# Two MLPs become streams of their own, stage A's mean matmuls take whole tiles, and the order is written anew

## The reference, cut to what matters

```python
x = _L0_xattn_ref(x, ctx_2048, ...)        # norm over all of (64, 256), 8 heads
x = _L1_xattn_ref(x, ctx_2048, ...)        # 16 heads, keys from the normed ctx
x = _L2_xattn_ref(ctx_2048, x, ...)        # keys from ctx and from x, then an MLP
x = _L3_xattn_ref(x, ctx_2048, ...)        # self attention, cross attention, MLP
...
mu = jnp.mean(input, axis=(1, 2), keepdims=True)      # layer 0
var = jnp.var(input, axis=(1, 2), keepdims=True)
...
out = rmsnorm(attn_out, postnorm_w)                   # layer 2
out = jax.nn.gelu(out @ mlp_w1 + mlp_b1) @ mlp_w2 + mlp_b2
return out + residual
...
ln_out = layernorm(x, ln3_s, ln3_b)                   # layer 3
mlp_out = gelu(ln_out @ w1 + b1) @ w2 + b2
return x + mlp_out
```

## Time and profile before

| what | value |
|---|---|
| time, median of 3 runs | 1334.38 us (1333.51 to 1335.9) |
| the profiled execution | 1336.17 us, its span 1334.1 us |
| TensorE busy | 1257.8 us, 94% |
| VectorE, ScalarE, GpSimd busy | 1041.4, 883.5, 568.4 us |
| mean granted TensorE clock | 0.98 of full |
| moved | 25.78 MB, mean 19 GB/s |

### The profile page before, as it was taken

The page is one execution under the profiler, slowest core; times in us unless marked ns, Lnnn a source line. Parts: engine busy times, 40 slices in busy tenths (PEclk is TensorE's granted clock), DMA queues, the critical chain, the costliest instruction groups (busy, mean ns, idle before and its releaser), DMA issues.

```text
span 1334.1 us, 35216 instructions
## 1 busy us (share of the span) xinstructions
PE 1257.8 (94%) x13116; PEld 964.1 (72%) x13116; DVE 1041.4 (78%) x2450; ACT 883.5 (66%) x2299; POOL 568.4 (43%) x977
## 2 busy tenths in 40 slices
PE   6999999999999999999999999999999999989675
PEld 4767678677686877777686777868777776868564
DVE  4778887878878788897888788787878778695753
ACT  3676666776875757676666866866677766756352
POOL 2552643463444436444454534444353453351421
PEclk9999999999999999999999999999999999989896
DMA  8100000000000000000000000000000000000000
GB/s 323 30 14 17 3 22 8 18 6 11 14 12 17 7 23 7 7 17 12 18 7 10 18 3 23 11 18 7 7 22 6 19 10 2 1 7 5 2 5 4
DMA packets 23589, 25.78 MB, mean 19 GB/s; under 512 B 10624, under 2 KB 22912, under 8 KB 23168
## 3 DMA queue, kind: packets, MB, share of 16 engines
q1 hardware_dynamic: 23424, 23.55, 5.6%
HBM read 21.44 MB, written 2.10 MB: 18 GB/s over the span
## 4 chain that ended last, share of the span: by engine, by line
PE 77%; DVE 9%; ACT 6%; issue 5%; POOL 2%; DMA 1%; SPq 0%; POOLq 0%; DVEq 0%; ACTq 0%
PE bank L678 9%; PE bank L504 8%; PE bank L944 8%; PE attended L633 8%; PE bank L953 8%; PE bank L618 7%; PE bank L712 5%; PE bank L684 5%; PE bank L493 4%; PE bank L738 3%; PE bank L701 3%; PE bank L725 3%; PE bank L671 2%; PE bank L415 2%; PE bank L729 2%
## 5 line engine op out<-in xcount | busy, mean ns | idle before, releaser
L605 POOL TENSOR_SCALAR p_a<-p_a,rec_a 128x256 f32<-128x256 f32 x512 | 245.8, 499 | 177.3 <-DVE rec_a L560 176.9
L591 ACT ACTIVATE p_a<-bank,nmax_a 128x256 f32<-128x256 f32 x512 | 237.5, 477 | 68.9 <-DVE nmax_a L554 68.1
L554 DVE TENSOR_REDUCE nmax_a<-bank 128x2 f32<-128x512 f32 x256 | 167.6, 679 | 13.0 <-PE bank L504 12.4
L618 PE MATMUL bank<-ident,p_a 128*128 128x128 f32 x1024 | 146.5, 278 | 8.7 <-POOL p_a L605 3.3
L504 PE MATMUL bank<-k_a,q_a 64*128 64x256 f32 x1024 | 141.6, 399 | 2.0 <-ACT p_a L666 0.6
L618 PEld LDWEIGHTS bank<-ident,p_a 128*128 128x128 f32 x1024 | 114.4, 142 | 39.8 <-issue 32.4
L633 PE MATMUL attended<-p_a,v_a 128*64 128x256 f32 x1024 | 135.0, 391 | 1.3 <-ACT p_a L666 1.3
L504 PEld LDWEIGHTS bank<-k_a,q_a 64*128 64x128 f32 x1024 | 90.6, 186 | 32.8 <-issue 24.6
L666 ACT ACTIVATE p_a<-bank 128x512 f32<-128x512 f32 x128 | 76.4, 600 | 52.3 <-PE bank L618 51.9
L591 ACT ACTIVATION_READ_ACCUMULATOR p_a<-bank,nmax_a 128x1 f32 x512 | 106.4, 208 | 0.0
L633 PEld LDWEIGHTS attended<-p_a,v_a 128*64 128x64 f32 x1024 | 64.2, 137 | 49.3 <-issue 21.3
(11 more groups left out here) (248 smaller groups left out, 3002.2 us busy)
## 6 DMA issues: line engine op xcount, KB each, us to landing
wb<-in_wb SPq DMA_DIRECT2D x1, 4096.0 KB, 12.8
wc<-in_wc SPq DMA_DIRECT2D x1, 4096.0 KB, 23.9
xc<-in_x SPq DMA_DIRECT2D x16, 128.0 KB, 2.7
xc<-in_ctx SPq DMA_DIRECT2D x16, 128.0 KB, 2.9
c_top<-in_ctx SPq DMA_DIRECT2D x16, 128.0 KB, 2.9
k_c<-in_ctx SPq DMA_DIRECT2D x16, 128.0 KB, 2.1
res_a<-in_x SPq DMA_DIRECT2D x16, 128.0 KB, 2.1
out<-y_out SPq DMA_DIRECT2D x16, 128.0 KB, 1.7
```

What stands on the lines that cost most here:

```text
L554: dve.tensor_reduce(nmax_a[:, n, e, :], ps[:, :].rearrange("p (q k) -> p q k", q=KT), AX.X, ALU.max, negate=True).then_inc(A.s["max"], 1)
L591: last = act.activation(p_a[:, j % 2, n, e, qt, :], ps[:, qt * D:(qt + 1) * D], ACT.Exp, bias=nmax_a[:, n, e, qt:qt + 1], accum_out=sum_a[ ...
L605: last = pool.tensor_scalar(p_a[:, j % 2, n, e, qt, :], p_a[:, j % 2, n, e, qt, :], rec_a[:, n, e, qt:qt + 1], 1.0, ALU.mult, ALU.mult)
L618: last = nc.tensor.transpose(ps[:, kt * D + qt * P:kt * D + (qt + 1) * P], p_a[:, j % 2, n, e, qt, kt * P:(kt + 1) * P], ident[:, :])
```

## The change

It has three parts. The MLP of E becomes a stage G and that of F a stage H, with own letters in the strings, own tiles for the hidden values (`g_hid`, `h_hid`), the normed input (`g_xn`, `h_xn`), its transpose and the residual; the sum `x6` gets a tile of its own too, and `wide` now lies in `qT`. The waits follow: what writes `x6` waits for G of the pair before, what writes `x5` for H. The two mean matmuls use a 128 x 128 tile of 1/64 with operands whose lower 64 partitions were set to zero once, at the start; the averages are read from the first 64 partitions as before. And `ORDER` and `BANK` are written anew. The title of the change says that the search for the order priced TensorE's changes of tile shape.

```diff
-    "e": (("xT",), ("q",), ("k",), ("v",)) + attention_fills(2) + (("nT0",), ("h0",), ("h1",), ("y",), ()),
+    "e": (("xT",), ("q",), ("k",), ("v",)) + attention_fills(2),
     "c": (("nT0",), ("q",), ("k",), ("v",)) + attention_fills(1),
-    "f": (("nT0",), ("q",)) + attention_fills(1) + (("nT1",), ("h0",), ("h1",), ("y",), ()),
+    "f": (("nT0",), ("q",)) + attention_fills(1),
+    "g": (("nT0",), ("h0",), ("h1",), ("y",), ()),
+    "h": (("nT0",), ("h0",), ("h1",), ("y",), ()),
...
-        "cbcccbceeeeeecccceeeeefeffeeeeefffckfcccfcfffccfccffffffffffff"),
+        "cbcehceeeehehcccceeeeefeffeggggffgfkfccchchchhccccfffffffhhhhh"),
...
-        mean_of_all = sb("mean_of_all", [S, S])
+        mean_of_all = sb("mean_of_all", [P, P])
...
-            T.wide = t("wide", [P, KT, P])
+            T.wide = T.qT
...
+        def mlp_tiles(T):
+            t = lambda n, shape: sb(f"{T.name}_{n}", shape)
+            T.hid, T.res = t("hid", [P, MT, P]), t("res", [P, D])
...
-        x2, x3, x4, x5 = (sb(f"x{n}", [P, D]) for n in range(2, 6))
-        x6 = E.xT[:, :, :].rearrange("p f q -> p (f q)")
+        x2, x3, x4, x5, x6 = (sb(f"x{n}", [P, D]) for n in range(2, 7))
...
-            filled(N, mm(ps[0:S, 0:2], mean_of_all[:, :], mv_a[:, :, 0], start=True, stop=True), i, "mean")
+            filled(N, mm(ps[:, 0:2], mean_of_all[:, :], mv_a[:, :, 0], start=True, stop=True), i, "mean")
...
+            if i == 0:
+                dve.memset(mv_a[S:P, :, :], 0.0)
+                dve.memset(small_a[S:P, :, :], 0.0)
...
+            def x6_free(eng):
+                if i:
+                    eng.wait_ge(G.s["xn"], G.at(i - 1, "xn", 1))
+            yield from pe_attention(E, i, ((K, ("v", 2)), (E, "v")), x6_free)
+
+        def pe_g(i):
+            yield from pe_norm(G, i, 0, "nT0")
```

More of the change, by code:

```diff
@@ L309, in norm_tiles @@
             T.stats, T.mv, T.eps, T.msq, T.rstd = t("stats", [P, 6]), t("mv", [P, 2]), t("eps", [P, 1]), t("msq", [P, 1]), t("rstd", [P, 1])
[L310 to L314, removed]
+            T.xnT = t("xnT", [P, KT, P])
+            T.xn = T.yT[:, :, :].rearrange("p f q -> p (f q)") if T is not K and T in (C, F) else t("xn", [P, D])[:, :]
         def attention_tiles(T, blocks):
@@ L427, in dve_n @@
             for n in range(2):
-                dve.bn_aggr(mv_a[:, n, :], stats_a[:, n, :]).then_inc(N.s["mv"], 1)
+                dve.bn_aggr(mv_a[0:S, n, :], stats_a[:, n, :]).then_inc(N.s["mv"], 1)
             yield
-            mean, dev, sq, var, eps, scale, shift, bias = (small_a[:, k, :] for k in range(8))
+            mean, dev, sq, var, eps, scale, shift, bias = (small_a[0:S, k, :] for k in range(8))
             ps = wait_fill(N, dve, i, "mean")
@@ L435, in dve_n @@
             written(N, dve, i, "mean")
-            dve.tensor_tensor(dev, mv_a[:, :, 0], mean, ALU.subtract).then_inc(N.s["dev"], 1)
+            dve.tensor_tensor(dev, mv_a[0:S, :, 0], mean, ALU.subtract).then_inc(N.s["dev"], 1)
             yield
@@ L786, in dve_attention @@
                 dve.wait_ge(T.s["res"], T.at(i, "res", 1))
-                residual = T.res[:, 0, :]
+                residual = T.res[:, :]
             ps = wait_fill(T, dve, i, "p")
@@ L866, in dve_norm @@
             dve.wait_ge(T.s["rstd"], T.at(i, "rstd", n + 1))
-            if n:
-                written(T, dve, i, f"nT{n - 1}")
+            if i and T in (G, H):
+                wait_fill(T, dve, i - 1, "nT0")
             if rms:
@@ L1078, in x3_free @@
                     eng.wait_ge(C.s["res"], C.at(i - 1, "res", 1))
-            yield from pe_mlp(E, i, WBt, "nT0", x3_free)
+            yield from pe_mlp(G, i, WBt, "nT0", x3_free)
         def dve_e(i):
@@ L1161, in pe_f, with x5_free, pe_h @@
             pe_project_T(F, i, "q", WCt["q1"], F.xnT)
-            yield from pe_attention(F, i, ((K, ("v", 4)),), lambda eng: None)
-            yield from pe_norm(F, i, 1, "nT1")
+            def x5_free(eng):
+                if i:
+                    eng.wait_ge(H.s["xn"], H.at(i - 1, "xn", 1))
+                    eng.wait_ge(H.s["res"], H.at(i - 1, "res", 1))
+            yield from pe_attention(F, i, ((K, ("v", 4)),), x5_free)
+        def pe_h(i):
+            yield from pe_norm(H, i, 0, "nT0")
             def stored_before(eng):
@@ L1167, in stored_before @@
                     eng.wait_ge(stored, 16 * i)
-            yield from pe_mlp(F, i, WCt, "nT1", stored_before)
+            yield from pe_mlp(H, i, WCt, "nT0", stored_before)
         def dve_f(i):
```

235 lines of the change are left out of this document (124 added, 111 removed).

## The result

The changed kernel takes 1304.26 us, median of 4 runs (1303.31 to 1305.18), against 1335.14 us (1333.51 to 1336.49) for the kernel before.

The account below looks back on a forecast made before the run. TensorE's own list was taken as the bound, with a softmax-and-norm chain in the last 100 us. Terms -8.0 + 3.2 - 3.5 - 1.5 - 3.0 = -12.8 us gave 1321.6 us from the median, range 1306 to 1336.

Parts of the forecast that it names:

- Fewer changes of shape: Along TensorE's list, 773 changes of shape become 687, 86 at 0.093 us each: -8.0 us.
- The mean matmuls: The 32 products on whole 128*128 tiles take up to 0.10 us more each on TensorE: +3.2 us.
- Work moved into the gaps of the end: In the last pair, 5.9 us of work moves behind E's begin, where TensorE idles: net -3.5 us.
- the clock: In the last pair's stretch from E on, a busier TensorE may keep 2.4 GHz rather than 1.2: -1.5 us.
- Own streams and tiles: MLPs and tiles freed from E of the next pair; only TensorE's waits can change: -3 us, bounds -15 and +25.
- ScalarE's loads: 12 fewer table loads on ScalarE, 15.4 us less work there, hidden beside VectorE's work: nothing, 3 us at most.
- Rival 1: B's softmax becomes a wait in every pair, 1.7 us in each of 15 pairs: +25.5, 1347 us; chance 0.12.
- Rival 3: TensorE's waits in the middle go too, 14.8 us of idle time instead of 3: 1310 us; chance 0.14.

Follow-up runs that it names:

- the pairs of runs above: New kernel plus 48 small matmuls: 1322.64 us with 87 added shape changes, 1316.57 with none; new order with 66 TensorE exchanges: 1340.24 us with more changes, 1331.33 with none.
- The three parts apart: Four runs: before's order in the new kernel 1334.53 us; new order with old tiles 1303.82; kernel before with whole-tile means 1334.48; new kernel with 64 x 64 means 1306.91.
- the run above: The kernel before with the whole-tile mean matmuls alone: 1334.48 us, ratio 0.9991.
- 66 neutral exchanges: 66 exchanges of neighbouring TensorE steps leaving the number of shape changes as it was: 1331.33 us in the new kernel, 1362.32 in before's order in the new kernel.
- the one with shared tiles: The new kernel with its order, but G and H hidden in E's and F's tiles as before the change: 1303.82 us, ratio 0.9764.
- a repair of eleven waits: Before's order in the new kernel, with the 11 longest-waiting TensorE steps moved behind the next one or two steps: 1339.35 us, ratio 1.0031.

## Why the prediction was wrong, point by point

I account for before's order in the new kernel (old) against the kernel after (new) by TensorE's own work at dense rates (1131.7 us in both), the changes of shape at the full price below, and the rest, which is waits of any kind, those too that a busy row hides. Stretches are by work done; they are cut at whole steps, so that some tenths move between them.

| stretch of work, us | changes, old | new | rest, old | new |
|---|---|---|---|---|
| 0 to 200 | 22.6 | 19.0 | 14.1 | 15.3 |
| 200 to 600 | 41.4 | 38.0 | 5.8 | -6.8 |
| 600 to 1000 | 40.4 | 36.6 | 7.6 | 3.3 |
| 1000 to 1080 | 4.5 | 5.2 | 5.8 | 6.0 |
| 1080 to the end | 2.1 | 2.4 | 50.2 | 45.9 |

(A rest below zero says that the rates taken are a little high there; both orders use the same.) The changes give 9.8 us and the rest 19.6, of which 16.9 between 200 and 1000 us of work. This is an account by list prices, not an experiment: in the pairs of runs above, changes of shape cost some 60 to 75% of their list price (6.1 us for 8.1, about 9 for 14), so the share of the waits may be larger still. The clock can't be a large part of the rest. In the profile of before's order in the new kernel it is at half for 44.3 us in all, of which 3.4 ahead of 1200 us, and in the kernel after for 34.5; even with TensorE at work throughout, 9.8 us less at half the clock return at most 4.9.

*Fewer changes of shape, -8.0.* The mechanism and the count are right, the price isn't. 0.093 us is only the exit; entry costs 0.055 us ahead of transposes and about 0.10 us ahead of float32 matmuls. For the 53 changes that the order saves the price of the exit alone gives 4.9 us, the full one 9.8. For the 33 of the mean matmuls it is the other way: as the rows of "The three parts apart" show, a whole-tile step pays an entry and an exit of its own where its neighbours have other shapes.

*The mean matmuls, +3.2.* From the upper bound I took the wrong end: 0.15 us to the next start against 0.12 is +1 us for 32. The reading of the load rows was wrong (141 ns is the load of a transpose), but the number wasn't made from it. With their 33 changes (-3.1) I had put the whole part at +0.1 us. The rows give -0.8 and the old order measured -1.2 (interval -2.7 to +0.3): two errors that nearly cancel. L406 to the next start also isn't always 0.12 to 0.22, as I had asked: it takes 0.15 between equal shapes, and L404 took 0.32 between two others in the run above.

*Work moved into the gaps of the end, -3.5, and the clock, -1.5.* Together they brought nothing from the last pair's B on, but not for want of the mechanism. E to the end grew by 3.4 us, with about 5.8 us of work more by the dense rates behind E's begin (5.9 had been counted); the idle time there fell by 1.6 us, and the mean granted clock rose from 0.79 to 0.83. What I hadn't seen is that TensorE then idles 1.8 us more between B and E. In the account by work it depends on the cut: from 1050 us of work on both orders take 134.6 us, from 1000 on the new one takes 3.1 us less, from 1080 on 4.0. E's MLP (L953 at 1231.75) runs 5.37 us, part of it at the lower clock as before, and f_sum (6.03 us), the norms and the last MLP follow each other as before.

*Own streams and tiles, -3.* **This is the step that failed.** The heading was wrong: the tiles do nothing. The term under it, "only the waits can change", was the largest of all, about -20 us instead of -3. I had taken a tenth of the 29.65 us of idle time, and had bounded it at -15; but for the low end of the range I used only -10 of it. With the bound as stated the end would have been 1301 instead of 1306, and 1304 inside it. The idle rows fell by 12.9 us, and more was hidden in busy rows than I allowed for. I compared the distances of producers and consumers by their medians and smallest values, and those came out mixed; here they didn't tell a 1334 us order from a 1304 us one. The runs show how much the exact places are worth (27 us for 66 neutral exchanges), not which of the places in the new order bring its 20 us; that stays open.

*ScalarE's loads, at nothing.* Right within the 3 us that were allowed for: removing 77 of 78 gives 2.6 us. But that isn't the whole of it. A load that the order doesn't know of cost 0.9 us of its 1.283, the small gelus included.

*The rivals.* Rival 1 did not come: TensorE waits at L721 for `b_sum` once, for 1.6 us, though the distance is the forecast 6.83. Rival 3 was nearest; its mark (idle below 18 us from 100 to 1190 us) came, with 16.2, at 1304 instead of 1310. Its reason, an order made with true prices, isn't shown, and that the neutral exchanges cost as much in the old order speaks rather against it.

**What stays open.** That the search's prices are what made the waits of the middle 17 us smaller, rather than more or luckier searching, can't be told from these runs: that needs strings made by the same search with the old prices. Nor was an order tried in which one engine keeps the old string and the others have the new one, and each recipe of exchanges was run with one set of places. Of the variants that change neither a function nor a softmax's guard, none beats the kernel after; the one with shared tiles equals it and spends less memory.

## What to carry to other kernels

Price the whole of a change of tile shape on TensorE, its exit and its entry, by start-to-start distances of the same group in both surroundings, before counting changes, and look at the neighbours on both sides: a narrow matmul given the commonest shape saves only where they have it. Where an order is fitted over several engines, be slow to forecast it by parts or to mend it: 66 harmless exchanges cost 27 us here, a repair of eleven waits cost 4.8, and only the whole new order paid. And test a resource by adding to it and by removing it, without moving a step, since the two gave 0.9 us and 0.03 us for the same table load.

## What the hardware showed unexpectedly

A change of tile shape costs 0.093 us behind the last matmul of the old shape and 0.055 (transposes) to 0.10 us (float32) ahead of the first of the new one. Behind a matmul of two columns of the same shape, 0.08 us of the 0.10 is paid as well. The weight load of a float32 matmul takes 109 to 113 ns for 32 columns (L725 of the kernel before), 131 to 137 for 64, and 189 to 198 for 128 in most groups, but a transpose's load of 128 columns takes 141. In the profile of the kernel after, TensorE's clock was at half only from 1214.5 us on; in that of the kernel before it also fell for 3.4 to 6.8 us at 28.9, 168.8 and 1189.4 us. That isn't a property of the order: with the new one it fell at 690.0 us in the run with ten loads more, and at 136.9 and 365.6 us in the one with twelve more.
